# A fused decoder layer on one core: the sort's slots one period later, and variance, bias blocks and first gates moved off VectorE and ScalarE

## The reference, cut to what matters

```
x = x + attn(layernorm(x))          # 16 batches, 128 rows each, D = 128; 16 heads of 8, causal blocks
x = x + xattn(layernorm(x), ctx)    # K and V by the matrix of the row's bucket (8 buckets), masked by times
y0 = layernorm(x)                   # then _L0_ffn_ref(y0):
y1 = _ln(y0 + _mha(y0), g1, b1)     # attention over the 16 batches at one position, 4 heads
gates = softmax(y1 @ wg); idx = argmax(gates)          # 8 experts
loc = place of the row among the rows of its expert; keep = loc < 256
y  = (y1 @ w1[idx] + b1[idx]) @ w2[idx] + b2[idx]      # no nonlinearity between
y2 = _ln(y1 + where(keep, gate * y, 0), g2, b2)
x = x + y2
```

## Time and profile before

| what | value |
|---|---|
| time, median of 3 | 338.67 us (338.23 to 341.26) |
| the profiled execution's own time | 339.11 us |
| its span in the profile | 337.3 us |
| busy PE / DVE / ACT / POOL | 319.2 / 261.2 / 166.6 / 126.0 us |
| chain that ended last | PE 73%, DVE 10%, issue 8%, POOL 5% |
| granted PE clock, mean | 0.981 |

### The profile page before, as it was taken

The page is one execution under the profiler, slowest core; times in us unless marked ns, Lnnn a source line. Parts: engine busy times, 40 slices in busy tenths (PEclk is TensorE's granted clock), DMA queues, the critical chain, the costliest instruction groups (busy, mean ns, idle before and its releaser), DMA issues.

```text
span 337.3 us, 12339 instructions
## 1 busy us (share of the span) xinstructions
PE 319.2 (95%) x4780; PEld 219.0 (65%) x4780; DVE 261.2 (77%) x661; ACT 166.6 (49%) x458; POOL 126.0 (37%) x208
## 2 busy tenths in 40 slices
PE   7869999999999999999999999999999999998994
PEld 3425556666666556565565665657666769898994
DVE  6874578866667789998899999875555638879996
ACT  2223545666666446455465564645425546733331
POOL 1063555100000254645423534234700005814896
PEclk9976999999999999999999999999999999999998
DMA  4972230636456163589556000000000000044412
GB/s 109 300 201 87 70 138 25 181 113 150 144 166 163 50 177 90 157 194 226 163 145 193 3 4 2 2 6 1 2 2 4 2 2 0 6 126 132 152 30 66
DMA packets 38697, 31.89 MB, mean 95 GB/s; under 512 B 4968, under 2 KB 36208, under 8 KB 38512
## 3 DMA queue, kind: packets, MB, share of 16 engines
q1 hardware_dynamic: 36064, 27.37, 28.9%
q0 software_dynamic: 1280, 3.15, 3.8%
q10 hardware_dynamic: 1296, 0.59, 0.7%
HBM read 23.40 MB, written 7.70 MB: 92 GB/s over the span
## 4 chain that ended last, share of the span: by engine, by line
PE 73%; DVE 10%; issue 8%; POOL 5%; ACT 1%; DMA 1%; POOLq 0%; DVEq 0%
PE ps L1328 9%; PE ps L1311 9%; PE ps L1274 8%; PE ps L1248 3%; PE ps L1227 3%; PE ps L1284 3%; PE ps L1361 3%; PE ps L1240 3%; PE ps L1399 3%; PE ps L1698 2%; PE ps L1344 2%; PE ps L1417 2%; PE ps L1218 2%; PE ps L1437 2%; POOL room L913 2%
## 5 line engine op out<-in xcount | busy, mean ns | idle before, releaser
L969 ACT ACTIVATE pT<-ps 128x512 f32<-128x512 f32 x128 | 73.9, 612 | 89.4 <-PE ps L1284 81.8
L837 POOL TENSOR_TENSOR rstd<-veps,minus_half 128x1 f32<-128x1 f32 x32 | 18.8, 586 | 117.2 <-DVE veps L452 117.1
L487 DVE TENSOR_REDUCE m_pad<-ps 128x8 f32<-128x1024 f32 x32 | 39.1, 1222 | 19.4 <-PE ps L1311 19.2
L463 DVE TENSOR_TENSOR p_sb<-qk_sb,heads 128x512 f32<-128x512 f32 x64 | 45.0, 705 | 0.9 <-ACT qk_sb L984 0.5
L490 DVE TENSOR_REDUCE m_pad<-ps 128x8 f32<-128x1024 f32 x32 | 38.9, 1216 | 0.0
L1274 PE MATMUL ps<-p_sb,qk_sb 32*128 32x512 f32 x256 | 38.1, 667 | 0.0
L1311 PE MATMUL ps<-p_sb,qk_sb 32*128 32x512 f32 x256 | 37.5, 656 | 0.0
L1328 PE MATMUL ps<-pT,p_sb 128*32 128x128 f32 x1024 | 35.1, 276 | 0.2 <-issue 0.2
L1284 PE MATMUL ps<-mT,negsel 32*128 32x128 f32 x512 | 33.0, 365 | 0.4 <-issue 0.4
L1698 PE MATMUL ps<-mexp,pT 128*128 128x128 f32 x256 | 31.9, 278 | 1.2 <-DVE pT L784 0.9
L1284 PEld LDWEIGHTS ps<-mT,negsel 32*128 32x128 f32 x512 | 21.3, 192 | 16.2 <-issue 16.2
(11 more groups left out here) (203 smaller groups left out, 682.0 us busy)
## 6 DMA issues: line engine op xcount, KB each, us to landing
room<-mask_rows SPq DMA_DIRECT2D x32, 128.0 KB, 3.4
wkv_sb<-wkv SPq DMA_DIRECT2D x23, 128.0 KB
kv_sorted<-room SPq DMA_DIRECT2D x5, 512.0 KB, 3.1
w1t_sb<-w1t SPq DMA_DIRECT2D x8, 256.0 KB
w_sb<-w SPq DMA_DIRECT2D x8, 256.0 KB
kv_sb<-hot_rows SPq DMA_DIRECT2D x4, 512.0 KB, 5.4
ctx_sorted<-room SPq DMA_DIRECT2D x1, 1472.0 KB, 10.3
tk<-fside SPq DMA_DIRECT2D x1, 1024.0 KB
```

Source lines behind the costliest of these rows:

```text
L463: return dve.tensor_tensor(dst, rows.unsqueeze(1).broadcast_to([128, QUADS, S]), heads[:, 0, :].unsqueeze(2).broadcast_to([128, QUADS, S]) ...
L487: dve.tensor_reduce(m4[:, 0:2, 0:QUADS], ps[:, 0:2, :].rearrange("p g (j k) -> p g j k", j=QUADS), AX.X, ALU.max).then_inc(s["max_low"], 1)
L837: pool.tensor_tensor(rstd[:, :], veps[:, :], minus_half[:, :], ALU.pow)\
L969: act.activation(pT[:, t % 2, g, :, :], quad[4 + g], ACT.Exp).then_inc(s["exped"], 1)
```

## The change

In the loop of periods: `bucket_tiles` and `bucket_slots` leave DVE's period -1 and stand in period 0, behind `norm_rows(4)`; the scatters are made in periods 0 to 5 (2, 3, 3, 3, 3, 2) in place of -1 to 4 (4, 3, 3, 2, 2, 2); `pad_masks` goes from period 4 to 5, `cross_masks(b)` from b + 5 to b + 6. `SORT_FROM` stays 6. SP starts the load of `ctx` before it waits for the constants, and no longer after.

In the expert stage: for batches 0 to 11 the sum of z's row comes out of the z instruction itself (`accum_out`), `less_rows` makes sum - 128 z on ACT from it, a new ACT instruction `row_squares` gives the sum of squares, and DVE's `squares_variance` makes the variance of a pair from that, one step later than `pair_variance` did; `z_stats` and `pair_variance` are left for batches 12 to 15. Bias blocks 8 to 15 go to GpSimd. Of `route_gates(0)` DVE keeps one instruction (room under the capacity, times the pick); the sums, the reciprocal (a power) and the products are nine GpSimd steps, `first_gates`.

```diff
-SCATTERS = (range(0, 4), range(4, 7), range(7, 10), range(10, 12), range(12, 14), range(14, 16))
+SCATTERS = (range(0, 2), range(2, 5), range(5, 8), range(8, 11), range(11, 14), range(14, 16))
...
             sp.dma_start(x_sb[:, 1:4, :], x[1:4].rearrange("b s d -> s b d")).then_inc(s["x_more_in"], 16)
+            sp.dma_start(ctx_sb[:, :, :], ctx.rearrange("b s d -> s b d")).then_inc(s["ctx_in"], 16)
             sp.wait_ge(s["heads_in"], 16)
             sp.wait_ge(s["sort_in"], 48)
             sp.wait_ge(s["consts_in"], 32)
-            sp.dma_start(ctx_sb[:, :, :], ctx.rearrange("b s d -> s b d")).then_inc(s["ctx_in"], 16)
...
-                if p == -1:
-                    bucket_tiles()
...
-                    bucket_slots()
...
                     norm_rows(p + 4)
+                if p == 0:
+                    bucket_tiles()
+                    bucket_slots()
...
-                if 0 <= p - 5 < B:
-                    cross_masks(p - 5)
+                if 0 <= p - 6 < B:
+                    cross_masks(p - 6)
...
+            def squares_variance(b):
+
+                dve.wait_ge(s["squared"], b + 1)
+                dve.tensor_scalar(ve16[:, b - 1:b + 1], zsquares[:, b - 1:b + 1], float(D), EPS * D * D, ALU.mult, ALU.add)\
+                    .then_inc(s["ve_ready"], 1)
...
                 if m == 1:
-                    route_gates(0)
+                    dve.wait_ge(s["place_done"], 1)
+                    dve.scalar_tensor_tensor(r_b[:, half(0), :], batches(bank[6]), float(CAP), pick_bf[:, 0, half(0), :],
+                                             ALU.is_lt, ALU.mult).then_inc(s["room_known"], 1)
...
+                    if b < B - 4:
+                        dve.scalar_tensor_tensor(z16[:, b, :], bank[4 + b % 2][:, 0:D], gate[:, b:b + 1], y1[:, b, :],
+                                                 ALU.mult, ALU.add, accum_out=zsum[:, b:b + 1]).then_inc(s["z_ready"], 1)
...
+                    if b % 2 == 0 and 2 <= b <= B - 4:
+                        squares_variance(b - 1)
+                    if b == B - 3:
                         pair_variance(b, 1)
...
-                if -1 <= p < 5:
-                    for b in SCATTERS[p + 1]:
+                if 0 <= p < 6:
+                    for b in SCATTERS[p]:
                         scatter_ctx(b)
-                if p == 4:
+                if p == 5:
                     pad_masks()
...
-            for b in range(B - 6, B):
+            def bias_block(b):
+
+                pool.wait_ge(s["cblk_ready"], max(b, B // 2))
+                pool.tensor_scalar(cblk[:, b, :], crep[:, :], batchof[:, b:b + 1], None, ALU.mult)\
+                    .then_inc(s["cblk_ready"], 1)
+
+            def gate_step(ins, step):
+                ins.then_inc(s["gate_step"], 1)
+                pool.wait_ge(s["gate_step"], step)
+
+            def first_gates():
+
+                n = half(0)
+                pool.wait_ge(s["gexp_ready"], 1)
+                halves = lg[:, n, :]
+                gate_step(pool.tensor_tensor(halves[:, :, 0:4], halves[:, :, 0:4], halves[:, :, 4:8], ALU.add), 2)
+                gate_step(pool.tensor_tensor(halves[:, :, 0:2], halves[:, :, 0:2], halves[:, :, 2:4], ALU.add), 3)
+                gate_step(pool.tensor_tensor(gate[:, n], halves[:, :, 0], halves[:, :, 1], ALU.add), 4)
+                gate_step(pool.tensor_tensor(gate[:, n], gate[:, n], minus_one[:, :], ALU.pow), 5)
+                pool.wait_ge(s["room_known"], 1)
+                room_left = r_b[:, n, :]
+                gate_step(pool.tensor_tensor(room_left[:, :, 0:4], room_left[:, :, 0:4], room_left[:, :, 4:8], ALU.add), 6)
+                gate_step(pool.tensor_tensor(room_left[:, :, 0:2], room_left[:, :, 0:2], room_left[:, :, 2:4], ALU.add), 7)
+                gate_step(pool.tensor_tensor(r_s[:, n], room_left[:, :, 0], room_left[:, :, 1], ALU.add), 8)
+                pool.tensor_tensor(gate[:, n], gate[:, n], r_s[:, n], ALU.mult).then_inc(s["gate_ready"], 1)
+
+            gate_step(pool.memset(minus_one[:, :], -1.0), 1)
+            for b in range(B - 6, B - 2):
                 y1_row(b)
+            for b in range(B // 2, B - 4):
+                bias_block(b)
+            first_gates()
+            for b in range(B - 2, B):
+                y1_row(b)
+            for b in range(B - 4, B):
+                bias_block(b)
...
-                act.activation(z16[:, b, :], z16[:, b, :], ACT.Identity, scale=-1.0, bias=mv16[:, b, 0:1])\
+                act.wait_ge(s["z_ready"], b + 1)
+                act.activation(z16[:, b, :], z16[:, b, :], ACT.Identity, scale=-float(D), bias=zsum[:, b:b + 1])\
                    .then_inc(s["c_ready"], 1)
+
+            def row_squares(b):
+
+                act.wait_ge(s["c_ready"], b + 1)
+                if b >= 2:
+                    act.wait_ge(s["squared"], b - 1)
+                act.activation(offs[:, b % 2, :], z16[:, b, :], ACT.Square, scale=1.0 / D, accum_out=zsquares[:, b:b + 1])\
+                   .then_inc(s["squared"], 1)
...
-            for b in range(8, B):
-                bias_block(b)
             turned_picks(1)
             turned_picks_exact(1)
             gate_exps(1)
             for i in range(B // 2 - 2):
                 for b in (2 * i, 2 * i + 1):
                     less_rows(b)
+                for b in (2 * i, 2 * i + 1):
+                    row_squares(b)
                 for b in (2 * i, 2 * i + 1):
                     by_root(b)
```

More of the change, by code:

```diff
@@ L171, in decoder_kernel @@
         ve16 = sb("ve16", [128, B])
+        zsum = sb("zsum", [128, B])
+        zsquares = sb("zsquares", [128, B])
+        offs = sb("offs", [128, 2, D])
+        minus_one = sb("minus_one", [128, B // 2])
         half16 = sb("half16", [128, B])
@@ L210, in decoder_kernel @@
             f_exped f_den_done f_ln_done f_rden_ready f_pv_done aT_ready f_proj_done z_ready w_ready y1_ready
-            y1T_done y1T_copied logits_done route_step shifted gexp_ready pick_ready gate_ready place_done
-            pickT_done pickT_copied picks_clear cblk_ready y1_rooted c_ready u_ready out_step last_rows pair_summed pair_rows hot_out hot_in_2 hot_in_3 hot_in_4 hot_in_5 hot_in_6 hot_in_7 xb_ready hot_done gated ffn_done out_rows""".split()
+            y1T_done y1T_copied logits_done route_step shifted gexp_ready pick_ready gate_ready room_known gate_step place_done
+            pickT_done pickT_copied cblk_ready y1_rooted c_ready squared u_ready out_step last_rows pair_summed pair_rows hot_out hot_in_2 hot_in_3 hot_in_4 hot_in_5 hot_in_6 hot_in_7 xb_ready hot_done gated ffn_done out_rows""".split()
         assert len(names) == len(set(names))
@@ L757, in route_picks, with route_gates @@
                 route(dve.tensor_reduce(r_m[:, n], r_b[:, n, :], AX.X, ALU.max))
-                dve.wait_ge(s["picks_clear"], 1)
+                dve.wait_ge(s["y1_ready"], 1)
                 dve.tensor_tensor(pick_bf[:, h, n, :], r_b[:, n, :], bcast(r_m[:, n]), ALU.is_equal)\
                    .then_inc(s["pick_ready"], 1)
-            def route_gates(h):
-                n = half(h)
-                dve.wait_ge(s["gexp_ready"], h + 1)
+            def route_gates():
+                n = half(1)
+                dve.wait_ge(s["gexp_ready"], 2)
                 route(dve.tensor_reduce(r_s[:, n], lg[:, n, :], AX.X, ALU.add))
                 route(dve.reciprocal(gate[:, n], r_s[:, n]))
-                dve.wait_ge(s["place_done"], h + 1)
-                route(dve.tensor_scalar(r_b[:, n, :], batches(bank[6 + h]), float(CAP), None, ALU.is_lt))
-                route(dve.tensor_tensor(r_b[:, n, :], r_b[:, n, :], pick_bf[:, h, n, :], ALU.mult))
+                dve.wait_ge(s["place_done"], 2)
+                route(dve.scalar_tensor_tensor(r_b[:, n, :], batches(bank[7]), float(CAP), pick_bf[:, 1, n, :],
+                                               ALU.is_lt, ALU.mult))
                 route(dve.tensor_reduce(r_s[:, n], r_b[:, n, :], AX.X, ALU.add))
@@ L809, in _ @@
                     dve.wait_ge(s["y1_ready"], b + 1)
-                    dve.scalar_tensor_tensor(z16[:, b, :], bank[4 + b % 2][:, 0:D], gate[:, b:b + 1], y1[:, b, :],
-                                             ALU.mult, ALU.add).then_inc(s["z_ready"], 1)
-                    z_stats(b, 1)
-                    if b % 2 and b < B - 2:
+                    if b < B - 4:
+                        dve.scalar_tensor_tensor(z16[:, b, :], bank[4 + b % 2][:, 0:D], gate[:, b:b + 1], y1[:, b, :],
+                                                 ALU.mult, ALU.add, accum_out=zsum[:, b:b + 1]).then_inc(s["z_ready"], 1)
+                    else:
+                        dve.scalar_tensor_tensor(z16[:, b, :], bank[4 + b % 2][:, 0:D], gate[:, b:b + 1], y1[:, b, :],
+                                                 ALU.mult, ALU.add).then_inc(s["z_ready"], 1)
+                        z_stats(b, 1)
+                    if b % 2 == 0 and 2 <= b <= B - 4:
```

(4 more changed lines are left out.)

25 lines of the change are left out of this document (12 added, 13 removed).

## The result

The changed kernel takes 349.39 us (348.71 to 350.48, six runs), the kernel before beside it 338.24 us (336.29 to 341.26): ratio 1.0348, 95% interval 1.031 to 1.0386. It is slower by 11 us; 343.0 us were forecast. The profiled execution takes 349.11 us of its own, its span is 347.0 us, against 339.11 and 337.3 before.

A forecast was written before the change was run, and what follows sets the result against it. PE was taken as the bound, at work in 319.2 of 337.3 us. The terms summed as 339.1 - 4.6 + 2.1 + 0.3 + 4.8 + 1.7 = 343.4, as a median 343.0 us; range 337 to 349.

The forecast's parts named there:

- The start: First 30 us: ACT's stand and the low PE clock behind it go, 5.3 less 0.7 for slots: 4.6 us gained.
- I take it that the stand came from there: ACT's stand at 21 to 23 us comes from the sort's traffic and goes: `turn_max(1)` 2.3 us earlier.
- I charge 0.7: Period 0: slot work mostly fits DVE's idle 4.17 us; with a faster start the next maxima come 0.7 us late.
- The scatters: Period 6: late last scatters make PE stand 2.5 us for the sorted rows; net +2.1 us (1.0 to 3.0).
- The masks: Period 21: DVE has `y0_rows` and `cross_masks(15)` together, 0.5 us on an engine with 0.3 free: +0.3 us.
- Gates and bias blocks: Expert stage: GpSimd's gates queue behind the wait for ACT's eighth block, delaying z(0) and `ffn(2)`: +3.7 us (+1.0 to +5.4).
- The clock there: Expert stage: PE's stand of 3.5 us before `ffn(2)` may bring the low clock level: +1.7 us.
- The sums: Expert stage: `squares_variance(1)` waits for ACT, `ffn(5)` 4.8 us late including the gates; later 0.4 gained and 0.4 lost.
- The tail as a whole: Expert stage: +4.8 us (+2.2 to +7) for gates and sums, and +1.7 for the clock.
- 4 (350): Rival, chance 0.05: ACT's stand stays and gates or clock cost their upper bounds, 350 us.
- 1 (347.6): Rival, chance 0.30: ACT's stand stays at 23 us, not caused by traffic; the start gains nothing, 347.6 us.
- its signs: Expected profile: ACT's exponential at 21.3, clock 1.00 from 22 to 30 us, period 6 stand over 2, GpSimd releasing z(0).

The follow-up runs named there:

- e5_before_again: The kernel before, unchanged, run and profiled once more: 331.3 us.
- f1_before_third: The kernel before, unchanged, run and profiled once more in a later session: 329.78 us.
- e1_front: The kernel before with only the first half of the change (slots, scatters, masks, `ctx` first): 338.36 us, ratio 1.0244.
- e7_front_slots_early: The kernel before with scatters and masks moved and `ctx` first, but bucket tiles and slots kept in period -1: 334.66 us, ratio 1.0102.
- e6_after_again: The changed kernel, unaltered, run once more against the kernel before: 345.59 us, ratio 1.0465.
- e2: The kernel before with only the second half of the change (sums, bias blocks, gates): 338.53 us, ratio 1.0232.
- e3_gates_first: The kernel before with the change's second half, but GpSimd makes the first gates ahead of bias blocks 8 to 11: 331.63 us, ratio 1.004.
- e8_gates_alone: The kernel before with only first gates and bias blocks 8 to 15 moved to GpSimd, gates first: 330.22 us, ratio 0.9985.
- e4_sums: The kernel before with only the variance by sums; bias blocks stay on ACT, first gates on DVE: 332.29 us, ratio 1.0052.

## Why the prediction was wrong

Terms for the profiled executions: predicted -4.6 + 2.1 + 0.3 + 4.8 + 1.7 = 4.3 us, measured 10.0.

*The start: predicted -4.6, measured +1.1 by `turn_max(7)`.* This is the step that failed, twice.

First, "I take it that the stand came from there [the sort's traffic] and goes". The stand did go from 21 us, and `turn_max(1)` came 4.2 us earlier. But such stands came back at 43.8 and 58.8 us, the second beside no traffic but scatters, and in five of seven sessions the kernel before took some 330 us; in the two of them in which it was profiled (`e5_before_again`, `f1_before_third`) it has none to lose. The gain was one of a session, not of the program. The warning was in the text ("no transfer is named as its releaser"), at 0.30; what it did not consider is that a wait without releaser can come back elsewhere. Nor did the traffic do it. `e5_before_again` has as much of it at the same time as the kernel before and its exponential starts in time, at 19.58 (stretches of `before`, then of `e5_before_again`):

```profile
20.00:22.00 2.00, 1.33 (x21) 0.92 (x13) 2.00 (x4) 0.00 (x0) 1.39 (x3) 0.77 0.38 110
22.00:24.00 2.00, 0.00 (x0) 0.00 (x0) 1.17 (x5) 0.60 (x1) 1.70 (x2) 1.00 0.59 188
```

```profile
20.00:22.00 2.00, 0.74 (x4) 0.58 (x5) 2.00 (x4) 1.05 (x4) 1.43 (x2) 1.00 0.40 108
22.00:24.00 2.00, 2.00 (x26) 1.34 (x28) 1.20 (x5) 1.59 (x5) 1.70 (x2) 0.52 0.69 187
```

Of the 4.2 us, 2.9 are what `e5_before_again` has without any change (`turn_max(1)` at 21.56 against 24.47). The other 1.3 come from the slots that left period -1, which the prediction put at nothing: without the stand PE waits there for DVE's maxima, 0.79 us in `e5_before_again`. Nor does the clock stay high behind short waits alone, as the prediction expected: in `e5_before_again` PE waited 0.91 and 0.79 us, was busy 0.74 of 2 us, and the granted clock then was 0.52 (rows above).

Second, "I charge 0.7" for the slot work. The cover was read off as the idle 4.17 us before the maxima at 29.34 in the trace of before, and most of that was the stand I had just removed. Without the stand DVE has 0.55 us there (`e5_before_again`), and the 3.5 us of slots stop PE for 2.4 to 3.0 us, with the low clock behind. `e1_front` against `e7_front_slots_early`, 1.0244 and 1.0102, prices it at some 4.7 us, more than the stand; the low clock is in that. By `turn_max(7)` the traces have 3.6 us (61.27 against 57.66), and 2.0 between `e6_after_again` and `e7_front_slots_early` (59.62).

*The scatters: predicted +2.1, measured +1.5 here*, 3.9 where PE comes earlier (`e7_front_slots_early`). The mechanism and the place were right, and in the changed kernel, where everything came late, the stand was short (1.29 us). The term left out that the low clock can follow this stand too: it does in `e7_front_slots_early`, for 1.8 us, and not in the changed kernel.

*The masks: predicted +0.3, measured +0.5.* From `turn_max(22)` to `turn_max(23)` pass 5.93 or 5.94 us in every trace with the masks as before (`before`, `e2`, `e3`, `e5`, `e8`, `f1`), and 6.45 to 6.50 in every one with the masks a period later (the changed kernel, `e1`, `e6`, `e7`). In `e6_after_again` PE waits 0.53 us there for DVE's maxima. No run moves the masks alone, but nothing else of the change lies there.

*Gates and bias blocks: predicted +3.7, measured +4.8* (`ffn(2)`, counted from `ffn(0)`: 10.83 us after `ffn(0)` against 6.05 before). The chain is the one described, from ACT's eighth block to z(0). Of its terms the gate steps were right (4.0 predicted, 3.75 measured, the power of eight columns 1.67 for 1.7); a bias block was sized as 0.33 and takes 0.60, 0.67 with its gap, because I took a copy as its nearest row. 4 x 0.27 = 1.1 us. `e3_gates_first` shows that their place ahead of the gates was all of this term and of the clock behind it.

*The clock there: predicted 1.7.* `ffn(2)` takes 3.75 - 2.03 = 1.72 us more and `ffn(3)` 2.48 - 1.95 = 0.53; a wait of 0.42 before `ffn(4)` goes, so that from `ffn(2)` to `ffn(4)` it is 1.8 more (6.57 against 4.74).

*The sums: predicted 4.8 - 3.7 = 1.1 for the tail beyond the gates, 0.4 - 0.4 later.* `e3_gates_first` against `e8_gates_alone` gives 1.24 + 0.23 = 1.5 us, `e4_sums` 1.9. Nearly right: the first wait costs PE 0.99 us, the loop through ACT, DVE and GpSimd gives nothing back.

The tail as a whole: predicted 6.5, measured 8.6 in the first comparison and 8.1 alone. The rivals: 4 (350) and 1 (347.6) came nearest in time, but both let the stand at 23 us stay, and it went; so their nearness is luck. The sign was right. The 5.7 us between 4.3 and 10.0 are 5.7 at the start and 2.1 in the tail, less 0.6 at the sorted rows, less 1.8 between `turn_max(8)` and `turn_max(31)` (predicted +0.3, measured -1.5; the kernel before lost 1.0 between `turn_max(14)` and `turn_max(15)` that the changed one did not), plus 0.3 outside the span.

Of its signs, z(0) was released by GpSimd and the clock fell behind it as said. ACT's first exponential came at 19.41 and not 21.3, the clock was not 1.00 up to 30 us, and PE's stand in period 6 was 1.29 and not over 2 us.

## What to carry to other kernels

Before you fill an engine's idle time, ask what made it: if it is the wait that your own change removes, it is no cover. Behind a wait that comes late in an engine's program put the work that nobody waits for last; here one exchange of two calls was worth 6.9 of 8.1 us. And a wait for which the profile names no releaser should not be booked as a gain on one profiled execution: take a second profile of the unchanged kernel first.
